# Second attention: the minus-maximum rows of a batch are moved ahead of the two row stores in SP's list

## The reference

```python
x = x + _L0_xattn_ref(_layernorm(x), ctx, Wq, bq, Wk, bk, Wv, bv)          # one head, width 256
x = x + _L0_ffn_ref(_layernorm(x), ...)                                     # three blocks of two linears
x = x + _L1_xattn_ref(ctx, _layernorm(x), w_q, w_kv, w_out, b_out)          # 16 heads of width 16
x = x + _L1_ffn_ref(_layernorm(x), norm1_w, w1, ..., norm2_w, w2)           # ternary weights, hidden 1024

# inside _L1_xattn_ref, per batch and head, q from x and k, v from the context:
attn = jnp.einsum('blhd,bshd->bhls', q, k) * SCALE
attn = jax.nn.softmax(attn, axis=-1)
out = jnp.einsum('bhls,bshd->blhd', attn, v)
```

## Time and profile before

| | us |
|---|---|
| median of 3 runs | 1247.68 |
| lowest, highest | 1246.42, 1248.28 |
| the profiled execution | 1247.51 |
| its span, first to last instruction | 1245.7 |
| PE busy | 1075.2 (86%) |
| DVE busy | 871.4 (70%) |
| ACT busy | 527.7 (42%) |
| POOL busy | 511.2 (41%) |

### The profile page before, as it was taken

How to read it: one execution, slowest core, us unless ns; L and a number is a source line. 1 busy time by engine, 2 the same in 40 slices (tenths; PEclk the granted TensorE clock), 3 DMA queues, 4 the chain that set the end, 5 groups by cost and what they waited for, 6 DMA issues and landing times.

```text
span 1245.7 us, 30741 instructions
## 1 busy us (share of the span) xinstructions
PE 1075.2 (86%) x9234; PEld 774.5 (62%) x9234; DVE 871.4 (70%) x2318; ACT 527.7 (42%) x953; POOL 511.2 (41%) x879
## 2 busy tenths in 40 slices
PE   7689999999999698989897589999999999766665
PEld 6567777777777466566653266666666666434444
DVE  4655565665665466676667589888888888378887
ACT  3312222222222111112114256565656665568886
POOL 1245444444444122221212225455445544566665
PEclk8889999999999799999999799999999999869998
DMA  8613333223232000000006577676777766540001
GB/s 225 167 49 94 93 93 91 86 84 86 86 92 80 19 1 0 0 0 0 1 1 130 123 162 152 143 160 152 155 151 161 155 150 145 182 153 21 25 26 34
DMA packets 121106, 116.08 MB, mean 93 GB/s; under 512 B 44867, under 2 KB 114022, under 8 KB 121062
## 3 DMA queue, kind: packets, MB, share of 16 engines
q1 hardware_dynamic: 121062, 115.54, 37.6%
HBM read 79.15 MB, written 36.00 MB: 92 GB/s over the span
## 4 chain that ended last, share of the span: by engine, by line
PE 44%; SPq 19%; DVE 15%; issue 9%; ACT 6%; DMA 3%; POOL 2%; DVEq 1%; POOLq 0%; ACTq 0%
PE bank L1558 25%; PE bank L1716 6%; SPq L514 6%; SPq L523 6%; PE bank L1652 3%; DVE nm L1323 2%; DVE hT L1255 2%; PE bank L1641 2%; PE bank L1920 2%; DVE yn L1244 2%; ACT v_all L1051 1%; SPq L553 1%; ACT v_all L1046 1%; POOL rs L740 1%; DVE v_all L1443 1%
## 5 line engine op out<-in xcount | busy, mean ns | idle before, releaser
L1323 DVE TENSOR_REDUCE nm<-bank 112x1 f32<-112x375 f32 x512 | 249.6, 538 | 15.4 <-PE bank L1799 13.6
L994 ACT ACTIVATE pT<-bank 125x448 f32<-125x448 f32 x384 | 185.4, 543 | 66.7 <-PE bank L1828 66.1
L1799 PE MATMUL bank<-ks,qs 96*128 96x375 bf16 x512 | 164.0, 332 | 18.3 <-DVE nm L1323 11.7
L1828 PE MATMUL bank<-qs,ks 128*128 128x112 bf16 x1536 | 137.7, 213 | 10.4 <-DMA qs<-mrow 10.1
L1828 PEld LDWEIGHTS bank<-qs,ks 128*128 128x128 bf16 x1536 | 110.3, 99 | 35.1 <-issue 10.3
L1842 PE MATMUL bank<-pT,vaug 125*32 125x112 f32 x3072 | 100.1, 263 | 0.0
L945 ACT ACTIVATE yT<-bank,bcol,gcol 128x448 f32<-128x448 f32 x48 | 32.1, 720 | 160.2 <-PE bank L1698 160.2
L1716 PE MATMUL bank<-wffT,hT 128*112 128x256 f32 x384 | 98.7, 391 | 0.0
L1558 PE MATMUL bank<-wv1T,ctxT 128*125 128x256 f32 x384 | 88.0, 379 | 0.0
L1558 PE MATMUL bank<-ctxT,wk1T 128*128 128x375 f32 x256 | 86.2, 479 | 0.0
L926 ACT ACTIVATE pr<-bank,ebias 112x375 f32<-112x375 f32 x32 | 18.3, 572 | 156.1 <-DVE ebias L1175 156.1
(11 more groups left out here) (206 smaller groups left out, 2326.7 us busy)
## 6 DMA issues: line engine op xcount, KB each, us to landing
k_parts_dram<-kp SPq DMA_DIRECT2D x192, 93.8 KB, 3.5
ks<-k_parts_dram SPq DMA_DIRECT2D x64, 281.2 KB, 4.1
cnat<-in_ctx_dram SPq DMA_DIRECT2D x32, 375.0 KB
ks<-k_parts_dram SPq DMA_DIRECT2D x64, 187.5 KB, 4.2
ks<-k_parts_dram SPq DMA_DIRECT2D x64, 93.8 KB, 3.9
q_parts_dram<-qp SPq DMA_DIRECT2D x48, 112.0 KB, 2.3
qs<-q_parts_dram SPq DMA_DIRECT2D x64, 84.0 KB, 3.5
x_stream<-in_x_dram SPq DMA_DIRECT2D x4, 896.0 KB, 13.5
```

The lines of the kernel that those rows point to most:

```text
L994: act.activation(pT[:, u % 6, :], B3[u % 3][0:TP], ACT.Exp).then_inc(probs_made, 1)
L1323: dve.tensor_reduce(nm[:, h:h + 1], scores[0:L], AX_X, ALU.max, negate=True).then_inc(head_max_taken, 1)
L1799: mm(A3[h % 2 if first else h % 3], qs[par][0:KS, h * L:h * L + P], ks[par][0:KS, h * T:(h + 1) * T], start=True, stop=True).then_inc(max_ ...
L1828: last = mm(B3[c][:, j * L:(j + 1) * L], ks[par][:, h * T + c * TP:h * T + c * TP + P], qs[par][:, h * L:(h + 1) * L], start=True, stop=True)
```

## The change

In `moves(b)` the call of `rows_m` moves from the head of the list to behind the two half loads, and takes the batch after: `moves(b)` now has `rows_m(b + 2)` where the next `moves` had it first. So in the row of all calls `rows_m(b + 2)` trades places with `store_y(b - 2)` and `store_x(b - 1)` alone, as long as nothing else stands at the end of `moves(b)`. `moves(0)` gets `rows_m(1)` as well.

```diff
             def moves(b, par):
 
                 more = not isinstance(b, int) or b < B - 3
-                if not isinstance(b, int) or b < B - 1:
-                    rows_m(b + 1, (par + 1) % 3)
+                if isinstance(b, int) and b == 0:
+                    rows_m(1, 1)
                 if more:
                     sp.wait_ge(shifted_scores_made, 12 * b + 6)
                     load_half(b + 3, par, 0)
                 if more:
                     sp.wait_ge(shifted_scores_made, 12 * b + 12)
                     load_half(b + 3, par, 1)
+                if not isinstance(b, int) or b < B - 2:
+                    rows_m(b + 2, (par + 2) % 3)
                 if not isinstance(b, int) or b >= 2:
                     store_y(b - 2)
                 if not isinstance(b, int) or b >= 1:
```

## The result

The changed kernel took 1253.56 us in the median of 7 runs (1250.84 to 1255.66), the kernel before in the same comparison 1247.68 us (1242.21 to 1249.53, 7 runs). The ratio is 1.0056 with a 95% interval of 1.0041 to 1.0071: 7.0 us slower, between 5.1 and 8.9. The forecast was 1256.0 us, within 1250.5 to 1261.5, slower.

A forecast was written before the change was run, and what follows sets the result against it. SP's DMA issue list was taken to bound the second attention at 11.17 us a round. 3.1 us there plus 5.2 us in the last rounds made 8.3 us, on 1247.68 giving 1256.0 us, range 1250.5 to 1261.5.

The forecast's parts named there:

- rival 1: Only the last rounds cost; in the loop SP's and PE's circles stay apart: 1252.9 us, chance 0.17.
- the stage: Second attention: 1.1 us once plus 2.0 us over some 22 rounds, together 3.1 us slower.
- SP's list is the clock of the rounds: Second attention from 831 us on: SP's back-to-back DMA issues set each round, 11.17 us.
- The load takes the place of the rows: Steady rounds: PE waits for loads instead of rows, starting 3.5 us after the rows' issue (T), not 2.4; 1.1 us once.
- Feedback between the two circles: Steady rounds: SP's and PE's near-equal circles wait for each other, some 0.1 us a round, 2.0 us.
- the short end: Steady rounds: new two-round circle of 22.2 us against SP's 22.34, so no cost from feedback.
- Part 2: Last rounds: late rows of batch 31 delay the second y tiles and the last stage's weights, 5.2 us.
- Early rounds nothing of their own: Early rounds, where SP waited for rows: longer wait, stores behind it, loads have a round's slack; no separate cost.
- rival 2: Only the second attention costs; the late weights are covered by something: 1250.8 us, chance 0.06.
- A longer stretch at the lower clock: Last stage: PE's longer pause may lengthen the low-clock stretch; not priced, widens the upper side of the range.
- Rival 3: Steady rounds: loads land later among the stores, another 0.25 us in each of 22 rounds: 1261.5 us, chance 0.12.
- rivals 4 and 5: Faster, PE's row waits go: 1243.0 us, chance 0.04; no change, gain offsets end or order is irrelevant: 1248.2 or 1247.7, 0.06.

The follow-up runs named there:

- e0: The changed kernel timed once more, nothing altered: 1251.94 us, ratio 1.0056 to the kernel before.
- e1: Changed kernel's order in all rounds, except that the rows of batch 31 stay at the head of the next moves: 1247.58 us, ratio 1.0013 to before.
- e5: Changed kernel with the last stage's weight loads issued ahead of the late stores and second y tiles: 1249.7 us, ratio 1.0025 to before.
- e6: Kernel before with ACT instead of SP issuing the loop batches' two stores, SP keeping those of the last batches: 1248.37 us, ratio 1.0019.
- e9: Kernel before with ACT issuing the loop's stores and POOL's norm waiting for DVE's row statistics: 1237.87 us, ratio 0.993.
- e11: Kernel before with only the added wait of POOL's norm for DVE's row statistics: 1245.92 us, ratio 0.9993.
- e2: Kernel before with only the rows of batch 31 brought forward into moves(29): 1249.17 us, ratio 1.003.
- e4: Kernel before with the last stage's weight loads issued ahead of the late stores and second y tiles: 1242.69 us, ratio 0.9969.
- e3: Kernel before with the two stores moved between the half loads, a batch later: 1283.73 us, ratio 1.0301.
- e8: Kernel before with stores between the half loads, a batch later, and POOL's norm waiting for DVE's row statistics: 1285.1 us, ratio 1.0315.

## Why the prediction was right

Right were the sign, the size and the split. The time alone would not have told: rival 1, only the end, gave 1252.9 us and is nearer to the measured 1253.56 than the forecast's 1256.0. It is the traces of after, e0, e1 and e5 that show the stage's part. Point by point:

- **SP's list is the clock of the rounds.** Shown by e6, e9 and e11 together: 11.17 becomes 10.83 when the stores leave the list and nothing else takes their place.
- **The load takes the place of the rows.** PE's start at T + 3.36 against 3.5, waits for qs<-mrow gone, those for qs<-q_parts_dram 8.9 us against "well over 8". Right.
- **Feedback between the two circles, 2.0 us taken from 0 to 3.** 11.28 to 11.34 a round where 11.17 was; T11 to T31 grew by 3.2 us, 2.3 of them up to T28 and 0.8 behind it, against 3.1 for the stage. SP's new row of waits, 1.3 us in 5 pieces of up to 0.3 (2.1, 1.6 and 1.5 in e0, e1 and e5), is this feedback: a little of nearly nothing, each time, and pieces under 0.15 us are in no such row. The choice off the short end was right; but the 0.1 us a round comes from a working that the prediction names and doesn't show, so how well 2.0 was hit is in part luck.
- **A reading that was wrong.** SP's waits for the rows were not "all before 831 us": the kernel before has another of 3.2 us at the rows of batch 31, which Part 2 itself relies on, and one of 1.3 us in 728 to 831 that stands at L553. For 831 to 1046 the reading holds.
- **Early rounds nothing of their own.** SP's wait for the rows in 728 to 831 grew from 7.9 us (6.6 and the 1.3 at L553) to 10.3, as foreseen, and T0 to T11 is 127.7 us on the mean of four kernels in the old order (before, e2, e4, e11) and 127.6 in the new one (after, e0, e1, e5). With 4 us from the shortest to the longest, that excludes a cost of several us, not one of 1 us.
- **The end, 5.2 us: 4.5 measured, two terms off in opposite directions.** The second y tiles were put at T + 8.7 and came at T + 9.2: the store of x 28 took SP 1.39 us to issue and released POOL 3.1 us after its start (1067.84 to 1070.93), where 1.9 was taken. That late, the store of y 28 (T + 6.9, forecast T + 6.0) had to wait only 2.3 us, so whether it was held doesn't show in the changed kernel; that stores behind large loads are held shows in e4 and e5. Nor does it matter there: the prediction left out that the second y tiles also wait for the landing of the first, T + 8.9 in the trace and T + 8.4 in its own sum, so a store that wasn't held could have saved no more than 0.3 us, and the 4.6 us for that case were out of reach. The burst from the second y tiles to PE was taken as unchanged, 10.8 us, and took 9.6 (1075.61 to 1085.20). It is 9.6 to 10.1 us in the three traces with late rows (after, e0, e2) and 10.5 to 10.8 in before, e1, e6, e9 and e11; why it is shorter no run tells apart. The weights at T + 18.8 are past the 17 that would have made the argument wrong.
- **A term that was missing.** The order in the loop delays the store of x 27 and with it the end by 1.7 us when it stands alone (e1). In the full change it lies under the wait for the rows of batch 31, so the sum didn't need it; rival 2, only the stage, should by the trace have had it.
- **A longer stretch at the lower clock**, left unpriced: nothing of it is seen. From PE's first transposes to the end it is 168.7 and 167.1 us in the two traces of the changed kernel, 167.2 in that of before, and the granted clock of the first 32 us of that is 0.58 and 0.53 against 0.52.

By the traces the sum is 3.2 + 4.5 = 7.7 us, forecast 8.3, timed 7.0 (5.1 to 8.9). Rival 2 (only the stage) falls with e2, by trace and by time. Rival 1 (only the end) falls by the traces, in which e1's rounds are long and e2's are not; by the times alone it would stand, as e1 is slower by 1.6 us with 0.0 within the interval. Rival 3 asked for rounds of 11.4 and more, which no trace of the new order has on the mean; rivals 4 and 5 fall with the time, and the gain on the rows that they count on doesn't come, since the load is late.

## What to carry to other kernels

When two things that one queue delivers both arrive just in time, handing one over earlier hands the other over later, and the pair settles a little above the longer circle: compute both circles before and after. Read the peeled last rounds apart from the loop; a wait that moved ahead of stores and loads there cost more (4.5 us, once) than the same move in all the rounds of the loop (3.2 us). And if a queue has been relieved and the time doesn't move, look at the single rounds and at the smallest instructions next to the work that the relief has shifted.

## What the hardware showed

**Small DVE instructions pay for POOL's long ones.** A 112x2 copy of 158 ns took 554 ns on the mean in e6, and casts and subtractions of 112x16 at 175 ns took up to 773 ns on the mean in e3; in the rows above they end within 0.05 us of the POOL instruction beside them, and in e8 one stood through two of them. The page "SBUF — State Buffer" of the Trainium skill (section "SBUF: two separate sides") says that GpSimd (POOL) shares a pair of ports with those DVE instructions that run in a mode with two ports or read two inputs from SBUF (the latter only against a GpSimd instruction that reads SBUF), and that whichever starts first has the pair for its whole instruction. The rows of e6 and e8 agree with such a lock; in which mode the copy and the casts run no trace shows. What the rows add is that it strikes through the phase: what releases POOL (the landing of a store in e8, DVE's last step on the maxima in e6) decides when it starts, and so what it meets.

**Issuing is not free where a round is many small DMAs.** A store costs SP 0.34 us and a rows move 0.83, a half load 2.03 + 1.86 of issues; with address work they make 11.17 us a round. The page "DMA: Bandwidth & Descriptors" (section "Issuing engines are not separate DMA queues") of the Trainium skill says that issuing from several engines saves only the time it takes to initiate a DMA, usually small relative to the DMA itself. Here it was 0.34 us of each round (e9), some 8 us of the kernel, once the collision was out of the way: e9 takes 1237.87 us, e11, which has the same wait and SP's stores, 1245.92.

**A small store behind large loads waits for them**: 5.9 and 7.4 us in e4 and e5, 6.6 in the kernel before, against a median of 2.1. The same page of the Trainium skill (section "Queues, rings and completion order") says that completion isn't first-in first-out for an issuing engine, and these rows show how little a late small store may gain from that.
